# Turning gathered rows by a DMA transpose instead of TensorE transposes and a copy

## The reference

```
x = x + attn(ln(x))      # "stage A": two quantised linear layers with SwiGLU between (rows of 1408)
x = x + xattn(ln(x))     # "stage B": token id picks one of 4 experts;
                         #   y = (silu(h @ C.T) * (h @ C.T)) @ C.T, C = ctx_2048[expert], 512 x 512
x = x + ffn(ln(x))       # "stage C": softmax router, top 2 of 8 experts (512 -> 352 -> 512, SwiGLU)
                         #   plus a shared expert of 704 for every token
```

## Time and profile before

| what | before |
|---|---|
| time, median of 3 runs | 934.32 us (933.33 to 942.64) |
| span of the profiled execution | 967.5 us, 17562 instructions |
| PE busy | 760.4 us (79%) |
| PE weight loads | 452.5 us (47%) |
| DVE, ACT, POOL busy | 504.4, 397.7, 263.6 us |
| stage B, first to last copy into hT | 283.3 to 393.9 us |
| routed part of C, first to last copy into hT | 617.5 to 870.0 us |

### The profile page before, as it was taken

One profiled execution on the slowest core, in us unless ns is written; L12 is line 12 of the kernel. 1 busy time (PEld: TensorE's weight loads), 2 busy tenths in 40 slices (PEclk: granted clock), 3 DMA queues, 4 the chain that ended last, 5 costly groups with the idle time before them and its releaser, 6 DMA issues.

```text
span 967.5 us, 17562 instructions
## 1 busy us (share of the span) xinstructions
PE 760.4 (79%) x5001; PEld 452.5 (47%) x5017; DVE 504.4 (52%) x861; ACT 397.7 (41%) x567; POOL 263.6 (27%) x401
## 2 busy tenths in 40 slices
PE   0457777777429999749778998899999999999275
PEld 0234443444215555335445655566666666665133
DVE  6779888887714555446564567222222222222146
ACT  5866556656515555335343543122332223231010
POOL 1235665565321111032121000111111111104710
PEclk9979899888559999969898999899999999999679
DMA  9312222212544555267776542122222222226843
GB/s 353 112 34 77 61 70 87 87 66 87 158 159 135 180 179 179 95 209 238 230 215 216 201 148 78 56 88 87 76 77 86 87 78 77 84 77 224 248 138 138
DMA packets 51204, 127.57 MB, mean 132 GB/s; under 512 B 6496, under 2 KB 6496, under 8 KB 50528
## 3 DMA queue, kind: packets, MB, share of 16 engines
q1 hardware_dynamic: 42688, 99.33, 30.5%
q0 software_dynamic: 8480, 27.79, 9.9%
HBM read 87.78 MB, written 39.32 MB: 131 GB/s over the span
## 4 chain that ended last, share of the span: by engine, by line
PE 47%; DMA 10%; issue 4%; another core or an unknown queue 4%; DVE 4%; SPq 2%; ACT 1%; POOL 0%; DVEq 0%; POOLq 0%; ACTq 0%
PE banks L1338 41%; DMA x_d<-w_hi 5%; PE banks L1330 3%; PE banks L1428 2%; DMA x_d<-yrow 2%; DMA hC_d<-w_lo 1%; PE banks L1360 1%; DMA rows<-hC_d 1%; DVE w_hi L1246 0%; DMA rows<-hC_d,idx 0%; SPq L458 0%; SPq L441 0%; DVE w_lo L1102 0%; DMA rows<-hB_d,idx 0%
## 5 line engine op out<-in xcount | busy, mean ns | idle before, releaser
L1338 PE MATMUL banks<-w_hi,hT 128*128 (+1 forms) x1288 | 321.0, 326 | 4.4 <-issue 3.2
L1338 PE MATMUL banks<-w_lo,hT 128*128 (+1 forms) x644 | 209.8, 326 | 0.0
L1338 PEld LDWEIGHTS banks<-w_hi,hT 128*128 128x128 f16 x1288 | 128.0, 99 | 82.2 <-issue 10.6
L1338 PE MATMUL banks<-w_hi,cpT 128*128 (+1 forms) x426 | 142.9, 390 | 10.0 <-issue 8.6
L1299 PE MATMUL banks<-w_hi,w_lo 128*128 128x352 bf16 x384 | 89.3, 350 | 45.6 <-DVE w_hi L1015 34.3
L844 ACT ACTIVATE cs<-banks 128x352 f32<-128x352 f32 x71 | 32.9, 463 | 201.7 <-PE banks L1338 175.5
L1160 DVE TENSOR_TENSOR cs<-banks,cs 128x352 f32<-128x352 f32 x71 | 37.1, 523 | 140.9 <-ACT cs L844 135.0
L1164 DVE TENSOR_TENSOR cpT<-banks,cpT 128x384 f16<-128x384 f32 x71 | 39.5, 556 | 129.3 <-ACT cpT L849 112.6
L1338 PE MATMUL banks<-w_lo,cpT 128*128 (+1 forms) x213 | 83.1, 390 | 5.3 <-issue 5.3
L1330 PE MATMUL banks<-eyeH,rows 128*128 128x128 f16 x584 | 47.6, 225 | 48.2 <-DMA rows<-hC_d 19.6
L1338 PEld LDWEIGHTS banks<-w_lo,hT 128*128 128x128 f16 x644 | 63.9, 99 | 34.5 <-issue 0.8
(11 more groups left out here) (191 smaller groups left out, 1214.3 us busy)
## 6 DMA issues: line engine op xcount, KB each, us to landing
wstage<-in_wmoe SPq DMA_DIRECT2D x40, 544.0 KB
yC_d<-yrow SPq DMA_DIRECT2D x39, 256.0 KB, 2.0
w_hi<-x_d SPq DMA_DIRECT2D x20, 256.0 KB
yB_d<-yrow SPq DMA_DIRECT2D x19, 256.0 KB, 2.0
w_hi<-in_wgate SPq DMA_DIRECT2D x3, 1408.0 KB, 9.9
w_hi<-in_x SPq DMA_DIRECT2D x16, 256.0 KB, 2.8
w_lo<-in_x SPq DMA_DIRECT2D x16, 256.0 KB, 3.6
x_d<-w_lo SPq DMA_DIRECT2D x16, 256.0 KB, 2.9
```

The source lines that it names most:

```text
L1338: mm = pe.matmul(to, a(k, pa), w(k, pw), start=(begins and k == 0 and n == 0), stop=(ends and k == steps - 1 and n == 2))
```

## The change

In stage B and in the routed part of C the eight transposes on PE and the copy on ACT are gone. SP issues one transposing DMA from `rows[u]` to `hT[u]` per tile, `b_turn` and `c_turn`, first in its list with lag -1. It waits for the gather (`b_rows`, `c_rows`) and for the product that last read the slot of `hT` (`b_t`, `c_gu`), and it raises `b_turned[u]` or `c_turned[u]` by 16 when it has landed. PE's product waits for that, and so does the gather of the tile two further on, which before waited for PE's turn. The shared half-tiles keep PE's transposes and ACT's copy.

```diff
@@ sp
-            pipeline(sp, J_B, [(-1, b_load, (0, W_B)), (1, b_store)])
+            def b_turn(s):
+                alone(sp, "sp", b_rows[s.u], (s.h + 1) * 16)
+                if not (isinstance(s.t, int) and s.t < 2):
+                    alone(sp, "sp", b_t, s.t - 1)
+                sp.dma_start_transpose(hT[s.u][:], rows[s.u][:]).then_inc(b_turned[s.u], 16)
+
+            pipeline(sp, J_B, [(-1, b_turn), (-1, b_load, (0, W_B)), (1, b_store)])
...
+            def c_turn(s):
+                alone(sp, "sp", c_rows[s.u], (s.h - (R0 // 2 - 1)) * 16)
+                if isinstance(s.t, int) and s.t == R0:
+                    alone(sp, "sp", c_gu, R0)
+                elif not (isinstance(s.t, int) and s.t == R0 + 1):
+                    alone(sp, "sp", c_gu, s.t - 1)
+                sp.dma_start_transpose(hT[s.u][:], rows[s.u][:]).then_inc(c_turned[s.u], 16)
...
-            pipeline(sp, TILES, [(1, c_store)], begin=R0, end=R1 - 2, kind=(R0, R1))
+            pipeline(sp, TILES, [(-1, c_turn, in_order), (1, c_store)], begin=R0, end=R1 - 2, kind=(R0, R1))
@@ pool
-                    alone(pool, "pool", b_T, s.t - 1)
+                    alone(pool, "pool", b_turned[s.u], s.h * 16)
                     alone(pool, "pool", b_rows[s.u], s.h * 16)
@@ act
-            pipeline(act, J_B, [(0, b_silu), (-1, b_evac), (0, b_split), (0, split_hi, (0, W_B))])
+            pipeline(act, J_B, [(0, b_silu), (0, b_split), (0, split_hi, (0, W_B))])
...
             def c_evac(s):
-                if rows_slot(s) != s.u:
+                if routed(s) or rows_slot(s) != s.u:
                     return
@@ pe
             def b_first(s):
-                pe.wait_ge(b_ev, s.t + 1)
+                pe.wait_ge(b_turned[s.u], (s.h + 1) * 16)
...
-            pipeline(pe, J_B, [(0, b_first), (-1, b_turn), (1, b_second), (0, b_turn_a)])
+            pipeline(pe, J_B, [(0, b_first), (1, b_second), (0, b_turn_a)])
...
             def c_gate_up(s):
-                pe.wait_ge(c_ev, results_before(s) + 1)
+                if routed(s):
+                    pe.wait_ge(c_turned[s.u], (s.h - (R0 // 2 - 1)) * 16)
+                else:
+                    pe.wait_ge(c_ev, shared_part(s)[0] + 1)
```

More of the change, by code:

```diff
@@ L328, in build @@
         w_in, whi_done, wlo_done = two("w_in"), sem("whi_done"), sem("wlo_done")
-        b_idx, b_rows, b_T, b_ev = sem("b_idx"), two("b_rows"), sem("b_T"), sem("b_ev")
+        b_idx, b_rows, b_turned = sem("b_idx"), two("b_rows"), two("b_turned")
         b_t, b_sil, b_a, b_aT = sem("b_t"), sem("b_sil"), sem("b_a"), sem("b_aT")
@@ L338, in build @@
         c_idx, c_shared, c_rows, c_T, c_ev = sem("c_idx"), two("c_shared"), two("c_rows"), sem("c_T"), sem("c_ev")
+        c_turned = two("c_turned")
         c_gu, c_sil, c_p, c_pT = sem("c_gu"), sem("c_sil"), sem("c_p"), sem("c_pT")
@@ L481, in c_rows_in @@
                 if isinstance(s.t, int) and tile == 1:
-                    sp.wait_ge(b_T, J_B)
-                sp.wait_ge(c_T, results_before(s))
+                    for u in range(2):
+                        sp.wait_ge(b_turned[u], 16 * ((J_B + 1 - u) // 2))
+                if s.first >= R1:
+                    sp.wait_ge(c_turned[1], 16 * (J_C // 2))
+                sp.wait_ge(c_T, tile)
                 sp.dma_start(rows[s.u][:], tiles(hC_d, tile)).then_inc(c_shared[s.u], 16)
@@ L514, in _ @@
             sp.wait_ge(b_y, J_B)
-            shared_first, shared_last = (0, R0), (R1, TILES)
+            shared_first, shared_last, in_order = (0, R0), (R1, TILES), (R0, R1)
             w_rest = (0, W_REST)
@@ L520, in _ @@
             pipeline(sp, TILES, [(W_LAG - 1, s_loadw, w_rest), (-2, c_rows_in, shared_first), (1, c_store),
-                                 (0, c_sum_in, shared_first)], begin=S_ROUNDS, end=R0, kind=(0, R0))
-            pipeline(sp, TILES, [(1, c_store)], begin=R0, end=R1 - 2, kind=(R0, R1))
+                                 (0, c_sum_in, shared_first), (-1, c_turn, (R0, R0 + 1))], begin=S_ROUNDS, end=R0, kind=(0, R0))
+            pipeline(sp, TILES, [(-1, c_turn, in_order), (1, c_store)], begin=R0, end=R1 - 2, kind=(R0, R1))
             def rows_of_pair(ap, pair):
@@ L543, in f_store @@
                 sp.dma_start(rows_of_pair(out, pair), tiles_of_pair(pair)).then_inc(f_out[odd], 16)
-            pipeline(sp, TILES, [(-2, c_rows_in, shared_last), (1, c_store), (0, f_load, summed_first),
+            pipeline(sp, TILES, [(-1, c_turn, in_order), (-2, c_rows_in, shared_last), (1, c_store), (0, f_load, summed_first),
                                  (0, c_sum_in, shared_last), (F_LAG, f_store, last)], begin=R1 - 2)
@@ L668, in c_gather @@
             def c_gather(s):
-                alone(pool, "pool", c_T, results_before(s) - (0 if isinstance(s.t, int) and s.t == R0 else 1))
+                if isinstance(s.t, int) and s.t == R0:
+                    alone(pool, "pool", c_T, R0 // SHARES)
                 if not (isinstance(s.t, int) and s.t < R0 + 2):
+                    alone(pool, "pool", c_turned[s.u], (s.h - R0 // 2) * 16)
                     alone(pool, "pool", c_rows[s.u], (s.h - R0 // 2) * 16)
@@ L790, in split_hi @@
                                scale=SCALE_C).then_inc(whi_done, 1)
[L792 to L795, removed]
             def b_silu(s):
@@ L831, in c_evac @@
             def c_evac(s):
-                if rows_slot(s) != s.u:
+                if routed(s) or rows_slot(s) != s.u:
                     return
-                act.wait_ge(c_T, results_before(s) + 1)
+                act.wait_ge(c_T, shared_part(s)[0] + 1)
                 if not (isinstance(s.t, int) and s.t == 0):
-                    two_ago = routed(s) and not (isinstance(s.t, int) and s.t == R0)
-                    act.wait_ge(c_gu, s.t - 1 if two_ago else s.t)
+                    act.wait_ge(c_gu, s.t)
                 act.copy(hT[s.u][:].rearrange("p a n -> p (a n)"), bank(0).bitcast(F16)).then_inc(c_ev, 1)
@@ L1394, in c_turn @@
                 if not (isinstance(s.t, int) and s.t == 0):
[L1395 to L1398, removed]
+                    pe.wait_ge(c_ev, shared_part(s)[0])
+                if s.first >= R1:
                     pe.wait_ge(c_shared[s.u], (shared_part(s)[0] - (R0 // SHARES - 1)) * 16)
```

## The result

The changed kernel takes 972.16 us (median of 3 runs, 969.09 to 976.1) against 934.32: 1.038 times as long, with a 95% interval of 1.030 to 1.046. It is slower by 38 us, where 914 had been forecast.

What follows compares the result with a forecast made beforehand. PE's order of work was taken to bound both stages. Rounds in B -1.9 us and C -17.1, starts +0.3 and -2.0, total -20.7: 934.3 to 914 us. Likeliest case 904 to 924; 8-in-10 range 903 to 1000.

Steps and rivals of the forecast that it cites:

- the sign: Whole kernel: faster by over 1% had 0.42, within 1% 0.14, slower 0.44; forecast change -20.7 us.
- the turn lands late: Rival, 33%: PE waits for turned rows ahead of each product; eight issues on SP, landing after 5.6 us, +34 us, 968.
- L: Time from the turn's issue on SP to its landing, taken from the gathers: 3.8 us in B, 3.4 in C.
- W + d: PE's work per round (5.61 us B, 5.96 C) plus how far into the round the turn is issued (2.5, 2.2).
- the formula: Both stages with a late turn: change = 9(8.11 + L) - 109.1 + 19(8.16 + L) - 243.6 + 2L - 8.9.
- P = (W + d + L)/2: Length of a round when PE waits for the turn: 5.955 us in B, 0.105 less than before.
- the start: From first gather's landing to first product: B 3.48 us before, +0.3 forecast; C 5.42 before, -2.0 forecast.
- slack: In C the turn was to land in 3.4 us where up to 3.8 would cost PE no wait.
- hidden: PE doesn't wait if the turn lands within 3.1 us of its issue in B, 3.8 in C.
- Does a chain that the transposes covered come out? Nothing comes out.: Between gate/up product and its result's transpose, silu and DVE's product keep slack: 1.17 us before, 0.72 after; no cost.
- What stands behind the turn on SP: B's weight load, wanted more than a round later, and the next store: both with room, no cost.
- The fall of the granted clock: In the late-turn rival: PE's gaps of about 1 us could also cost clock; no size given.

Runs made afterwards that it cites:

- loadfirst: The changed kernel with PE's register load of the expert number ahead of the wait for the turned rows: 952.74 us, ratio 1.020.
- the run again: The kernel before, run once more with no edit for a second profile: 934.88 us, ratio 0.998.
- removed: The changed kernel with neither transposes nor DMA turn; hT holds constants and the product waits for the gather: 918.39 us, ratio 0.980.
- before_early: The kernel before, transposes on PE, with the expert number loaded before the wait for the product's result: 931.22 us, ratio 0.995.
- ahead_early: The changed kernel with the turn one round earlier, ahead of the store, and the expert number loaded before the wait for the product's result: 907.49 us, ratio 0.970.
- ahead: The changed kernel with the turn one round earlier in SP's order, ahead of the store: 942.92 us, ratio 1.008.
- late_early: The changed kernel, turn still behind the store, with the expert number loaded before the wait for the product's result: 947.46 us, ratio 1.011.

## Why the prediction was wrong

**The range held, the sign did not.** The time lies in the rival "the turn lands late" (33%), near its worked value of 968; but for another reason than L = 5.6, so that this nearness is luck. The rival's place (the wait ahead of each product) and its chain (copy, store, turn) were right, and its price was not: L is 3.7 to 4.2.

**What bounds the kernel, and the structure of the round: right.** PE's order sets both stages. Two rounds are the product, the chain to SP's store, the turn's issue, L, and then the product again.

**W + d: nearly right.** In C the chain has 687.26 - 678.60 = 8.66 us from a product to the turn's issue in the next round, where 5.96 + 2.2 = 8.16 was taken. d itself is 2.26, by the timeline of the round, whose product starts at 685.00; the rest, 0.44, is W, which holds a gap of 0.37 us after line 1437. In B: 344.73 - 336.26 = 8.47, against 8.11.

**L: nearly right.** 4.2 against 3.8 in B; in C 3.7 by the median and 4.0 in the chain above, against 3.4. The Trainium skill, "VectorE: DVE Perf Modes", section "The three transpose paths", gives 1309 ns for one 128x128 turn by DMA, and eight of them in a row would be an estimated 10.5 us. The trace doesn't show them in a row: all eight in one DMA land in 3.0 to 4.9 us. With L as measured the formula gives 9 x (8.11 + 4.2) - 109.1 = +1.7 us in B and still -17.1 in C, since 3.7 is under 3.8: the forecast would have been 918, still faster. L was named as the number on which the sign hangs, and it wasn't.

**The step that failed: a late round ends when the turn lands.** The prediction wrote P = (W + d + L)/2. It is (W + d + L + R)/2, and R, the restart of PE behind the wait, is 1.14 us in the chain of both stages (0.94 to 1.38 in 54 of the 58 products); 0.85 of it goes when the register load is moved (loadfirst). In B, over 9 pairs of rounds, R is 10.3 us, W + d 3.2 and L 3.6: 17.1, with 1.6 more at the start (forecast +0.3; from the gather's landing at 281.29 to the product at 286.62 it is 5.33 us instead of 3.48). That is 18.7 us; B missed by 18.2. The near agreement is partly luck, since the terms are those of one pair and of a median: counted from product to product, the 18 rounds took 126.0 us (286.62 to 412.57) where 107.2 was forecast, and the end of the stage is 1.4 us shorter than in the run again. In C a pair was to take 2 x 5.96 = 11.92 and took 13.74 (2 x 6.87): 19 pairs are 34.6 us more. The start takes 8.7 us from the first gather's issue at 634.3 to the product at 643.03, as in the run again (614.9 to 623.60), where 2.0 less was forecast. That is 36.6 of the 37.3 us by which C missed. Of C's pair of 13.80, R is 1.14, L 0.6 over the value taken, the longer W 0.44 and d 0.06; the 0.36 of slack that the forecast had is used up by these. Without R a pair would be 12.66, less than the 12.82 of the kernel before: R is the largest term in both stages, though L and W also lie above what was taken. It shortens the slack too: hidden meant L of at most W - d - R, about 2.0 us in B and 2.6 in C, and not 3.1 and 3.8. With R alone added, the forecast's own rounds would have given 9 x (8.11 + 3.8 + 1.14) - 109.1 = +8.4 us in B and 19 x (8.16 + 3.4 + 1.14) - 243.6 = -2.3 in C: no gain.

**The second step that failed: "Does a chain that the transposes covered come out? Nothing comes out."** Only silu and the product on DVE were looked at. What came out was not a chain of other engines but PE's own register load. With no turn at all (removed) the rounds of C lose 0.15 us of the 0.45. With the load put early the 0.45 was right: 6.30 in before_early, 5.88 in ahead_early. So even a landing in time would not have given the forecast: ahead, in which PE waits for no turn in C, stands at 1.008.

**What stands behind the turn on SP, and the clock: right.** In the chain of two rounds shown for each stage there is no weight load, no store's landing and no gather; the stores of yC_d land later (3.0 us instead of 2.0), and nothing in the loop waits for them. The fall of the granted clock that the prediction named as a possible cost of PE's gaps came only at the start of C.

## What to carry to other kernels

Before work is taken off the bounding engine, ask what that work covered on the same engine: here the register loads and address work of the next product were not counted as busy, and appeared only as "issue" once the cover was gone. Behind a wait that may be late, put nothing but the work itself; load numbers and addresses ahead of it. And in a queue in order, a transfer that gates the bounding engine goes ahead of a store that waits for a late result: here the two moves together turn a loss of 4% into a gain of 3%.

## What the runs showed of the hardware

- A DMA that turns 256 KB of 16-bit rows from SBUF to SBUF holds SP for 1.23 to 1.51 us at its issue in the changed kernel, against 0.33 for a plain store and 0.48 for a plain copy from SBUF to SBUF of the same size. It lands after 3.0 us at best; the medians of a stage are 3.7 and 4.2 in the changed kernel and 3.1 in C of ahead. The plain copy lands after 2.3 us at best, with medians of 2.3 to 2.9.
- It moves in packets under 512 B: some 61,000 of them for 58 turns (plain copies instead: under 1,000 more than before). The DMA share in C is 0.46 in the changed kernel, 0.37 with plain copies in its place and 0.25 with neither (before and removed).
- A product whose weights are addressed by a register begins 0.94 to 1.38 us after its rows have landed if the register is loaded behind the wait (54 of the 58 products of the changed kernel), and 0.29 to 0.38 us after it if ahead (53 of the 58 of late_early).
- A register load of PE from SBUF takes 0.30 us at the median, and 0.41 (0.89 at most) in stage C of ahead; in ahead_early, with the same transposing DMAs, 0.32 at most. The cause is open.
- PE's gaps of up to 1.4 us in a round of 6.9 left the granted clock at 1.00, the level of 2.4 GHz (660 to 900 us of the changed kernel); right after a gap of 5.90 us it was 0.50, the level of 1.2 GHz, from 642.0 to 648.6 us.
